# Second layer: bias adds at the head of GpSimd's body, two score steps ahead of the output projection, key and query banks swapped

## What is computed

```python
xn = layer_norm(x, norm_w, norm_b)
q = (xn @ q_w + q_b).reshape(Bx, Tx, H, -1)
k = (xn @ k_w + k_b).reshape(Bx, Tx, H, -1)
att = jnp.einsum('bnhl,bmhl->bnmh', q, k)
att = jax.nn.softmax(att + (1.0 - mask) * -1000000.0, axis=2)
v = ((xn @ v_w + v_b) * src_mask[:, :, None]).reshape(Bx, Tx, H, -1)
y = jnp.einsum('bnmh,bmhl->bnhl', att, v).reshape(Bx, Tx, Dx)
h = layer_norm(y, sb_norm_w, sb_norm_b) * (1.0 + scale) + shift
return x + jax.nn.silu(h) @ out_w + out_b
```

## Time and profile before

| what | us |
|---|---|
| median of 3 runs | 2480.9 |
| lowest and highest of the runs | 2477.12 to 2482.09 |
| time of the profiled execution | 2484.31 |
| its span, first to last instruction | 2482.5 |
| PE busy in it | 2359.0 (95%) |
| DVE busy | 1557.4 (63%) |
| ACT busy | 823.2 (33%) |
| POOL busy | 601.7 (24%) |

### The profile page before, as it was taken

One profiled execution on the slowest core, in us unless ns is written; L12 is line 12 of the kernel. 1 busy time (PEld: TensorE's weight loads), 2 busy tenths in 40 slices (PEclk: granted clock), 3 DMA queues, 4 the chain that ended last, 5 costly groups with the idle time before them and its releaser, 6 DMA issues.

```text
span 2482.5 us, 43830 instructions
## 1 busy us (share of the span) xinstructions
PE 2359.0 (95%) x15670; PEld 2125.6 (86%) x15670; DVE 1557.4 (63%) x3441; ACT 823.2 (33%) x1893; POOL 601.7 (24%) x847
## 2 busy tenths in 40 slices
PE   7999999999999999968999999999999999999998
PEld 5888888888888888857989898998889898989897
DVE  4677777777777777654465655556565656555654
ACT  2233333333333333332333333333323333333332
POOL 0333333333333333232121212122221212121210
PEclk9999999999999999978999989999989999989997
DMA  6100000000000010014444434353524343433432
GB/s 238 72 34 35 36 35 34 34 34 34 34 34 34 34 35 34 25 47 95 105 96 111 94 91 114 86 120 86 120 73 115 90 117 89 117 83 100 105 93 54
DMA packets 90933, 187.14 MB, mean 75 GB/s; under 512 B 18708, under 2 KB 29394, under 8 KB 90904
## 3 DMA queue, kind: packets, MB, share of 16 engines
q1 hardware_dynamic: 88856, 186.23, 28.3%
q10 hardware_dynamic: 2048, 0.53, 0.1%
HBM read 51.81 MB, written 33.69 MB: 34 GB/s over the span
## 4 chain that ended last, share of the span: by engine, by line
PE 47%; DVE 5%; issue 2%; POOL 1%; DMA 0%; ACT 0%; DVEq 0%; POOLq 0%; SPq 0%
PE bank L1423 7%; PE bank L439 5%; PE bank L441 5%; PE bank L440 5%; PE bank L430 5%; PE bank L431 5%; PE bank L1413 4%; PE bank L432 4%; PE bank L1439 4%; DVE h_lo L1207 2%; DVE z L1176 1%; DVE stats_y L1181 1%; POOL ve_y L1073 1%; POOL rstd_y L1075 1%; PE bank L1372 1%
## 5 line engine op out<-in xcount | busy, mean ns | idle before, releaser
L439 PE MATMUL bank<-xT_hi,w_hi 128*128 128x256 f32 x1536 | 446.4, 291 | 2.6 <-DVE xT_lo L1145 1.4
L440 PE MATMUL bank<-xT_lo,w_hi 128*128 128x256 f32 x1536 | 448.1, 292 | 0.0
L441 PE MATMUL bank<-xT_hi,w_lo 128*128 128x256 f32 x1536 | 445.0, 290 | 0.0
L1154 DVE SCALAR_TENSOR_TENSOR parts<-bank,qk_bias,parts 128x256 fp32r<-128x256 f32 x256 | 112.1, 479 | 432.9 <-ACT parts L1284 432.9
L1423 PEld LDWEIGHTS bank<-v,prob 128*128 128x128 f32 x2048 | 317.6, 195 | 12.7
L430 PE MATMUL bank<-w_hi,xT_hi 128*128 128x512 f32 x768 | 317.0, 413 | 0.0
L432 PE MATMUL bank<-w_lo,xT_hi 128*128 128x512 f32 x768 | 314.6, 410 | 0.0
L431 PE MATMUL bank<-w_hi,xT_lo 128*128 128x512 f32 x768 | 314.4, 409 | 0.0
L439 PEld LDWEIGHTS bank<-xT_hi,w_hi 128*128 128x128 f32 x1536 | 293.2, 191 | 4.8 <-DVE xT_lo L1145 1.8
L440 PEld LDWEIGHTS bank<-xT_lo,w_hi 128*128 128x128 f32 x1536 | 293.3, 191 | 1.9
L1423 PE MATMUL bank<-v,prob 128*128 128x33 f32 x2048 | 293.3, 251 | 0.0
(11 more groups left out here) (163 smaller groups left out, 4232.9 us busy)
## 6 DMA issues: line engine op xcount, KB each, us to landing
stack<-parts SPq DMA_DIRECT2D x768, 128.0 KB
xr<-in_x SPq DMA_DIRECT2D x32, 512.0 KB, 3.5
x_between_layers<-x SPq DMA_DIRECT2D x64, 256.0 KB, 2.0
xr<-x_between_layers SPq DMA_DIRECT2D x32, 512.0 KB, 3.6
out<-y_out SPq DMA_DIRECT2D x64, 256.0 KB, 2.0
w_emb<-in_L_cond_W_emb SPq DMA_DIRECT2D x4, 1024.0 KB, 9.9
w_emb<-in_L_cond_emb_w SPq DMA_DIRECT2D x4, 1024.0 KB, 4.8
raw<-in_L_cond_Wq SPq DMA_DIRECT2D x1, 1024.0 KB, 5.5
```

Source lines behind the costliest of these rows:

```text
L439: yield nc.tensor.matmul(dst, w_hi[:, m, c, fs], a_hi[:, c], start=(first and c == 0), stop=False)
L440: yield nc.tensor.matmul(dst, w_hi[:, m, c, fs], a_lo[:, c], start=False, stop=False)
L441: yield nc.tensor.matmul(dst, w_lo[:, m, c, fs], a_hi[:, c], start=False, stop=(c == C - 1))
L1154: nc.vector.scalar_tensor_tensor(parts[:, LO[n], c].rearrange("p b t -> p (b t)"), ps[QK_BANKS[n][c // 2]][:, at:at + PAIR * P], qk_bias[: ...
```

## The change

Four things are edited, all in `layer1`.

- **GpSimd**: `biases(i + 1)` at the end of body i becomes `biases(i)` at the head of body i. The call for pair 0, which stood ahead of the bodies, goes into the first body.
- **Banks**: keys go to banks 2 and 3, queries to 0 and 1, values to 2 and 3. The scores of sequence 0 are written in bank order 0, 1, 2, 3, those of sequence 1 in the order 2, 3, 0, 1.
- **TensorE**: in front of the weaving of sequence 0 stand two steps of `scores(i, 0)` instead of three of `out_rows(i - 1, 0)`. The wait for the values moves to banks 2 and 3.
- **VectorE**: `values(i, 0)` goes ahead of `end_norm(i - 1, 1)`, `values(i, 1)` behind `low_part(i - 1, 0)`, the first `maxima` ahead of `end_silu(i - 1, 1)`, and the maxima of sequence 1 follow the new bank order.

```diff
-    QK_BANKS = ((2, 3), (0, 1))
+    QK_BANKS = ((0, 1), (2, 3))
-    V_BANKS = (0, 1)
+    V_BANKS = (2, 3)
+    S_ORDER = ((0, 1, 2, 3), (2, 3, 0, 1))
...
-        biases(0, 0, True)
         def body(i, first, more, last):
+            biases(i, i % RING, first)
             if not last:
                 norm(i + 1)
             if not first:
                 end_rstd(i - 1, 0)
                 end_gains(i - 1)
                 end_rstd(i - 1, 1)
-            if not last:
-                biases(i + 1, (i + 1) % RING, False)
...
+            values(i, 0, first)
+            if not first:
                 end_norm(i - 1, 1)
                 low_part(i - 1, 0)
-            values(i, 0, first)
             values(i, 1, first)
+            maxima(i, 0, (0,))
             if not first:
                 end_silu(i - 1, 1)
-            maxima(i, 0, (0,))
+            maxima(i, 0, (1,))
             if not first:
                 low_part(i - 1, 1)
-            maxima(i, 0, (1, 2))
+            maxima(i, 0, (2,))
...
-            maxima(i, 1, (0,))
+            maxima(i, 1, (2,))
             if not last:
                 x_low(i + 1, 1)
-            maxima(i, 1, (1, 2, 3))
+            maxima(i, 1, (3, 0, 1))
...
-                if b == 0 and j < 2:
-                    pe.wait_ge(s["v"], seq(PAIR, i, j + 1))
+                if b == 0 and j >= 2:
+                    pe.wait_ge(s["v"], seq(PAIR, i, j - 1))
...
-            outputs0, scores0 = () if first else out_rows(i - 1, 0), scores(i, 0, range(C))
+            outputs0, scores0 = () if first else out_rows(i - 1, 0), scores(i, 0, S_ORDER[0])
-            run(islice(outputs0, 3))
+            run(islice(scores0, 2))
             woven(outputs0, scores0)
-            outputs1, scores1 = () if first else out_rows(i - 1, 1), scores(i, 1, range(C))
+            outputs1, scores1 = () if first else out_rows(i - 1, 1), scores(i, 1, S_ORDER[1])
```

More of the change, by code:

```diff
@@ L1160, in maxima @@
             for j in banks:
-                dve.wait_ge(s["s_ps"], seq(PAIR * C, i, b * C + j + 1))
+                dve.wait_ge(s["s_ps"], seq(PAIR * C, i, b * C + S_ORDER[b].index(j) + 1))
                 nc.vector.tensor_reduce(top[:, b, :].rearrange("p (a c) -> p a c", c=C)[:, :, j],
@@ L1428, in scores @@
         def scores(i, b, banks):
-            if b == 0 and banks[0] == 0:
+            if b == 0:
                 pe.wait_ge(s["stack"], seq(16 * STACK_DMAS, i, 16 * STACK_DMAS))
             for j in banks:
-                if b == 0 and j < 2:
-                    pe.wait_ge(s["v"], seq(PAIR, i, j + 1))
+                if b == 0 and j >= 2:
+                    pe.wait_ge(s["v"], seq(PAIR, i, j - 1))
                 if b == 1:
```

## The result

The changed kernel takes 2502.4 us (2501.6 to 2503.0), the one before 2480.1 us in the same comparison: a ratio of 1.0095, interval 1.0078 to 1.0111. It is slower by 0.95%, where 2452 us was forecast and 2487 us was the end of the range. The profiled execution has a span of 2499.8 us, 17.3 us more than the one before. One execution of the kernel before, in a later comparison, took 4540 us, where all others took 2475 to 2497; it is in the slow state and left out everywhere.

What follows compares the result with a forecast made beforehand. TensorE, busy 95%, was taken as the bound. -0.45 + 0.54 = +0.1 us in 31 bodies (+3 us) and -31.7 us for the clock gave a median near 2452 us; own range 2446 to 2460, full range 2427 to 2487.

Steps and rivals of the forecast that it cites:

- Who bounds, and the exclusion: TensorE bounds, busy 95%; SBUF-heavy operations of VectorE and GpSimd exclude each other for a whole operation; VectorE's PSUM reads aren't held.
- The branch on GpSimd: Between rstd_y and the adds: the 0.2 us branch is covered, the add still starts before z(1); 0.
- v(0) ahead of z: On VectorE: v(0) takes 0.7 us where VectorE idles 0.71 us waiting for rstd_y; 0.
- Two score steps in front: At the score phase's start, four score products fill TensorE's wait for h_lo(0); -0.45 us per body.
- What is late next: In sequence 1's scores: v_bias starts before hs, so TensorE waits for maxima of banks 2 and 3; +0.54 us per body.
- The clock: TensorE's five clock falls after the score phase's idle times vanish, as 0.46 of 1.95 us idle is filled; -31.7 us.
- falls stay: Rival: TensorE's clock falls stay or come back elsewhere, leaving only +3 us; 2484 us, range 2476 to 2490; chance 0.16.
- slower by VectorE: Rival: VectorE bounds the score phase, TensorE waits 1.04 us for maxima; +18 us, 2499 us with falls as before; chance 0.09.

Runs made afterwards that it cites:

- e3: The changed kernel with GpSimd's mask copy and v_bias moved behind the second reduction; 2452.8 us, ratio 0.9894.
- e2: The kernel before with two more 256-column matmuls per body in front of the first key matmul; 2506.3 us, ratio 1.0085.
- e8: e3 with six more 256-column matmuls per body in front of the first key matmul; 2505.1 us, ratio 1.0088.

## Why the prediction was wrong

By its own steps:

- **Who bounds, and the exclusion.** Right. The runs with GpSimd out of the way show z(1) at 0.55 us, h_lo(0) at 0.69 us and no wait of TensorE for either; on the kernel before none is left at all. One part of it had no evidence: that v isn't held. In the rows v stands beside no wide operation of GpSimd; what they show is that the reductions aren't held.
- **The branch on GpSimd, 0.** Right: the add kept its 0.07 us, and the run with the biases back at the end is the same.
- **v(0) ahead of z, 0.** Right: z(1) starts at the same distance from rstd_y.
- **Two score steps in front, -0.45 us.** Right: -0.44 us by e3 against the kernel before. The wait for h_lo(0) is 0.63 us, 0.55 forecast.
- **What is late next, +0.54 us.** The mechanism was right in each link: mask copy 0.18 us (0.20 forecast), hs 1.42 us (1.4), the bank 2 scores 7.95 us after z(1) starts (7.94), the bank 3 scores 9.15 us after (9.13). The size was short by 0.12 us, +0.66 by the changed kernel against e3. TensorE's keys start 12.75 us after z(1), against 12.52 before. The score pair after each of the two waits takes 0.44 instead of 0.34 us, and the next matmul starts 0.27 to 0.28 instead of 0.17 us later. Here a stop costs 0.1 us more than the stop itself. In all +0.22 us per body instead of +0.1; 6.4 us instead of 3.
- **The clock, -31.7 us.** This is the step that failed. It came out at +10.9 us. The prediction said that "a pair of 1.5 us should not be" enough for a fall when 1.95 us was just enough. It took idle time as the measure, and the falls followed the length of a body: 17 falls at 41.47 us, 1 at 40.97 us, with the same idle times. Filling idle time with score products did not keep the clock up: at 41.5 us the falls add 42.5 us with the wait filled and 46.0 us without (e2, its slowest execution). Which bodies fall, and why, stays open.

The rival "falls stay" had 0.16 and its price was 2476 to 2490. It named in passing that a longer body could shift where the falls come, but held the number of falls at 5. The rival "slower by VectorE" had 0.09 and a price of 2499 us, which is near the measured 2502.4, but by luck. It needed 1.04 us of waiting per body; the two waits cost 0.66 us, and e8 has 14 falls without them. The stated range ended at 2487 and left this rival's price out.

The forecast of 2452 us comes back as the time of e3, 2452.8 us, by luck too: its body is 0.44 us shorter than before, and falls still add 15.8 us.

The trace before had the warning in it: alike idle times in all bodies and five falls means that something other than the idle time picks the bodies.

The Trainium skill says that activity releases the throttle (TensorE: Matmul & The Clock Gate, What's actually happening). The runs agree at one end: with TensorE busy throughout, the granted clock is 1.00 for 1138 us. It also says that a VectorE instruction with at most one SBUF input, outside the two-port modes, does not contend with GpSimd (SBUF — State Buffer, Who interferes with whom). The reductions agree: with the late GpSimd on the kernel before they take 0.68 us beside the adds and beside v_bias, as alone. For v the runs hardly test it: in the trace of the changed kernel it overlaps a wide operation once, at 0.75 us against 0.74.

## What to carry to other kernels

Where VectorE and GpSimd both work in SBUF, look for an operation that takes two to three times as long in most passes as in the one where the other engine has nothing to do: whoever starts first holds the other for a whole operation, so give GpSimd's wide work a semaphore that puts it beside VectorE's reductions of PSUM. Before filling a wait with work pulled forward, follow what the pulled operations release: v(1) came 0.66 us sooner, and that started v_bias ahead of the one operation that TensorE would want. A change of a few tenths of a microsecond in a periodic body can move the clock by more than its own size; take the clock term with both signs in the range unless the idle time goes altogether.

## What the hardware showed beyond that

- The number of clock falls depends on the length of the loop's body: 0.5 us less, in a dense part far from the idle times, took them from 17 to 1. Longer is not always more: 5 at 40.81 us, 1 at 40.97 us.
- A fall ends sooner with the new score phase (6.8 us, costing 2.35 to 3.2 us) than with the old one at 41.2 us and more (10 to 17 us, costing 4.8 to 7.9 us). In the shortened old one two of three falls last 3.4 us and cost 1.6 us.
- A taken loop branch on GpSimd's sequencer is free where an operation of 0.55 us runs ahead of it.
